# Causal attention on one core: the mask of the maxima added by TensorE, and the values of two halves issued together

## The reference

```
x = x + 0.5 * ffn(layernorm(x))
x = x + attention(layernorm(x))      # 16 heads of 16 features, causal
x = x + 0.5 * ffn(layernorm(x))

attention:  scores = Q K^T / 4, -inf where key > query
            softmax over keys, times V, heads summed through WO
ffn:        256 -> 1024, butterfly (10 stages), gelu, butterfly, 1024 -> 256
```

## Time and profile before

| | |
|---|---|
| time, median of 3 runs | 2121.79 us (2121.55 to 2124.14) |
| the profiled execution, its own time | 2122.12 us |
| its span, first to last instruction | 2120.3 us |
| busy: TensorE, VectorE, ScalarE, GpSimd | 96%, 79%, 64%, 12% |
| mean granted TensorE clock | 0.988 of full speed |

### The profile page before, as it was taken

How to read it: one execution, slowest core, us unless ns; L and a number is a source line. 1 busy time by engine, 2 the same in 40 slices (tenths; PEclk the granted TensorE clock), 3 DMA queues, 4 the chain that set the end, 5 groups by cost and what they waited for, 6 DMA issues and landing times.

```text
span 2120.3 us, 58107 instructions
## 1 busy us (share of the span) xinstructions
PE 2033.0 (96%) x23960; PEld 1207.5 (57%) x23960; DVE 1680.3 (79%) x3588; ACT 1350.4 (64%) x1592; POOL 259.0 (12%) x723
## 2 busy tenths in 40 slices
PE   1699999989999999999999999999999999999999
PEld 1476666555555555555555555555555555568887
DVE  6734444459999999999999999999999999635562
ACT  2423222238888888888888888888888888763222
POOL 8300000001111111111111111010110111100000
PEclk8799999999999999999999999999999999999999
DMA  7011211121211111111111111111111111101110
GB/s 202 22 48 47 86 52 51 47 61 44 51 42 45 41 43 49 42 46 41 44 47 42 46 43 44 46 42 46 43 44 45 42 46 33 50 24 60 60 40 21
DMA packets 89976, 104.19 MB, mean 49 GB/s; under 512 B 21264, under 2 KB 52592, under 8 KB 89456
## 3 DMA queue, kind: packets, MB, share of 16 engines
q1 hardware_dynamic: 89008, 100.23, 16.6%
q0 software_dynamic: 704, 0.25, 0.2%
HBM read 70.54 MB, written 29.36 MB: 47 GB/s over the span
## 4 chain that ended last, share of the span: by engine, by line
PE 92%; DVE 4%; ACT 2%; issue 1%; SPq 1%; DMA 0%; ACTq 0%; DVEq 0%
PE PS L1067 31%; PE PS L1189 30%; PE PS L1048 12%; PE PS L1025 6%; PE PS L1169 6%; PE PS L1120 3%; PE PS L1042 1%; DVE OA L781 1%; PE PS L991 1%; DVE BNS L718 1%; DVE OA L771 1%; ACT PG L606 0%; ACT L583 0%; SPq L367 0%; ACT OA L591 0%
## 5 line engine op out<-in xcount | busy, mean ns | idle before, releaser
L667 ACT ACTIVATE PG<-PS 128x1024 f32<-128x1024 f32 (+1 forms) x1152 | 1119.5, 978 | 248.0 <-PE PS L1169 186.3
L880 DVE TENSOR_REDUCE MXP<-PS 128x1 f32<-128x512 f32 x1792 | 1106.5, 686 | 35.7 <-PE PS L1067 34.8
L1067 PE MATMUL PS<-KT,QT 48*128 48x512 f32 (+3 forms) x2304 | 821.0, 431 | 5.6 <-DVE MXP L880 3.1
L1169 PE MATMUL PS<-QT,KT 50*128 50x512 f32 (+1 forms) x2304 | 810.0, 431 | 0.0
L1189 PE MATMUL PS<-PG,VH 128*17 128x128 f32 x16896 | 725.9, 276 | 0.1
L1189 PEld LDWEIGHTS PS<-PG,VH 128*17 128x17 f32 x16896 | 400.1, 96 | 414.5 <-issue 364.1
L1067 PEld LDWEIGHTS PS<-KT,QT 48*128 48x128 f32 x2304 | 345.8, 184 | 271.8 <-DVE MXP L880 129.9
L1169 PEld LDWEIGHTS PS<-QT,KT 50*128 50x128 f32 x2304 | 339.3, 184 | 10.3 <-issue 9.9
L876 DVE CUSTOM_DVE_ANT_0 PS<-PS,MASK 128x128 f32<-128x128 f32 (+3 forms) x512 | 249.9, 505 | 83.0 <-PE PS L1067 75.6
L551 POOL TENSOR_SCALAR_AFFINE_SELECT PG<-PG 128x128 f32<-128x128 f32 x512 | 137.3, 294 | 1005.4 <-ACT PG L667 1005.2
L1048 PE MATMUL PS<-MD,PG 128*128 128x256 f32 x1024 | 244.1, 388 | 4.9 <-DVE X L845 3.4
(11 more groups left out here) (101 smaller groups left out, 899.2 us busy)
## 6 DMA issues: line engine op xcount, KB each, us to landing
KT<-k_parts SPq DMA_DIRECT2D x256, 64.0 KB
QT<-q_parts SPq DMA_DIRECT2D x256, 64.0 KB
q_parts<-OA SPq DMA_DIRECT2D x16, 512.0 KB, 2.7
k_parts<-OA SPq DMA_DIRECT2D x16, 512.0 KB, 2.7
KT<-k_parts SPq DMA_DIRECT2D x256, 32.0 KB
QT<-q_parts SPq DMA_DIRECT2D x256, 32.0 KB
o_parts<-OS SPq DMA_DIRECT2D x128, 64.0 KB
OA<-o_parts SPq DMA_DIRECT2D x32, 256.0 KB
```

The costliest lines, as they stand in the source:

```text
L667: nc.scalar.activation(PB[n % 2][half][:, :, q0:TILE], PS[:, half * 1024:half * 1024 + 1024].rearrange("p (k q) -> p k q", k=2)[:, :, q0:T ...
L880: nc.vector.tensor_reduce(dst, bank(b), AX.X, ALU.max).then_inc(mx_red, 1)
L1067: mm(bank(4 + qs % 2 if b is None else b, w), NQ[0:SC, (BT * place(j) + qs) * P:(BT * place(j) + qs + 1) * P].bitcast(f32r), NK[0:SC, c * ...
L1169: last = mm(PS[:, (2 * half + k) * 512 + q0:(2 * half + k + 1) * 512], CK[0:SM, kb * P:(kb + 1) * P].bitcast(f32r), CQ[0:SM, place(j) * TI ...
```

## The change

In attention TensorE adds the causal mask to a diagonal maximum: behind the matmul of the maximum, which leaves its accumulation open, comes a second matmul into the last 128 columns, the bf16 identity (identb) times the 128 x 128 triangle of MASK. VectorE then reduces it with a plain tensor_reduce of (qs + 1) x 128 columns. The 28 diagonal maxima made before attention keep VectorE's masked instruction.

The second half of the values of a chunk moves one slot on, to just before the first half of the next chunk's values, so that both are issued together; only for the last chunk of a query tile (c = 0, ends_tile) it stays at the end of its slot. pv_done becomes two semaphores, one for each half, and each exponential waits for its own.

```diff
-        pv_done = sem("pv_done")
+        pv_done = [sem("pv_done0"), sem("pv_done1")]
...
+        def ends_tile(n):
+
+            return CH[n % NCH][1] == 0
@@ GpSimd, copy_v @@
-                    pool.wait_ge(pv_done, (h - 1) * NCH + CH.index((NT - 1, c)) + 1 + FREE_PB)
+                    pool.wait_ge(pv_done[1], (h - 1) * NCH + CH.index((NT - 1, c)) + 1 + FREE_PB)
@@ ScalarE, exps and take_sums @@
-                act.wait_ge(pv_done, h * NCH + n + 1)
                 for half in range(2):
+                    act.wait_ge(pv_done[half], h * NCH + n + 1)
...
-                act.wait_ge(pv_done, h * NCH + LAST[j] + 1 + FREE_PB)
+                act.wait_ge(pv_done[1], h * NCH + LAST[j] + 1 + FREE_PB)
@@ VectorE, maximum @@
-                b = 4 + qs % 2 if b is None else b
+                first = b is None
+                b = 4 + qs % 2 if first else b
                 dve.wait_ge(mx_ps, seq + 1)
                 dst = MXP[:, BT * place(j) + qs, c:c + 1]
-                if j == c:
-                    w = (qs + 1) * P
+                w = (qs + 1) * P if j == c else TILE
+                if j == c and first:
...
-                    nc.vector.tensor_reduce(dst, bank(b), AX.X, ALU.max).then_inc(mx_red, 1)
+                    nc.vector.tensor_reduce(dst, bank(b, w), AX.X, ALU.max).then_inc(mx_red, 1)
@@ TensorE, maximum @@
-                mm(bank(4 + qs % 2 if b is None else b, w), NQ[0:SC, (BT * place(j) + qs) * P:(BT * place(j) + qs + 1) * P].bitcast(f32r),
-                   NK[0:SC, c * TILE:c * TILE + w].bitcast(f32r), start=True, stop=True).then_inc(mx_ps, 1)
+                dst = bank(4 + qs % 2 if b is None else b, w)
+                alone = j != c or b is None
+                last = mm(dst, NQ[0:SC, (BT * place(j) + qs) * P:(BT * place(j) + qs + 1) * P].bitcast(f32r),
+                   NK[0:SC, c * TILE:c * TILE + w].bitcast(f32r), start=True, stop=alone)
+                if not alone:
+                    last = mm(dst[:, qs * P:(qs + 1) * P], identb[:, :], MASK[:, 3 * P:4 * P], start=False, stop=True)
+                last.then_inc(mx_ps, 1)
@@ TensorE, values @@
-                if half:
-                    last.then_inc(pv_done, 1)
+                last.then_inc(pv_done[half], 1)
@@ TensorE, the loop over slots @@
                 ahead_maximum(n, 1)
+                if n > 1 and not ends_tile(n - 2):
+                    values(*divmod(n - 2, NCH), 1)
                 if n:
                     values(*divmod(n - 1, NCH), 0)
...
                 ahead_maximum(n, 3)
-                if n:
+                if n and ends_tile(n - 1):
                     values(*divmod(n - 1, NCH), 1)
```

More of the change, by code:

```diff
@@ L975, in _ @@
             pe.sem_inc(y_ps, 1)
-            pe.sem_inc(pv_done, FREE_PB)
+            for half in range(2):
+                pe.sem_inc(pv_done[half], FREE_PB)
             pe.wait_ge(a_up, 1)
```

## The result

The changed kernel takes 2303.81 us (2301.76 to 2306.87, 4 runs) beside 2121.67 us before: ratio 1.0857, 95% interval 1.0838 to 1.0876. It is 182 us slower; the forecast was 194 slower, 2316, in a range of 2250 to 2360.

What follows compares the result with a forecast made beforehand. The prediction took TensorE's order to set the pace, with VectorE just behind. From 2122 us it took 148 for the merge, added 136 for the bank wait and 206 for the masks: 2316 us, range 2250 to 2360.

Steps and rivals of the forecast that it cites:

- The merge: Attention's values of two halves issued together save 0.33 us in each of 448 slots, a slot of 2.12 us: -148 us.
- a TensorE that waits for exponentials: Sign of being wrong: in the profile after, idle ScalarE is replaced by TensorE waiting for exponentials.
- The bank wait: Fourth maximum in a row waits for the first's reduction in three banks, 0.59 us at 230 slot borders: +136 us.
- the wait view: Sign of being right: idle time of TensorE's maxima loads put down to VectorE's reductions grows by over 100 us.
- The masks: Full-height mask matmuls break the groups of pairs in 121 diagonal slots, 3.82 us each, 1.70 over 2.12: +206 us.
- the term m: Time of a mask from its load to the next load in masked slots: 0.215 us, bounds 0.14 and 0.25.
- VectorE's relief: Dropping 484 masked maxima and their accumulator reads frees 60 us of VectorE in slots where it waits already: 0.
- Banks that don't hold TensorE: Rival: in the merged order VectorE keeps pace with bursts of maxima, so no bank wait: 2180 us; chance 0.08.
- Masks that don't break groups: Rival: in diagonal slots a mask costs its 0.05 us and pairs stay together: 2134, up to 2200 us; chance 0.05.
- VectorE as the limit: Rival: VectorE limits masked slots and its relief pays -0.5 us x 121 = -60: 2062 us; chance 0.04.
- More waits than counted: Rival: row transposes in the long groups, or masked slots with late exponentials, add waits: 2360 us and over; chance 0.03.

Runs made afterwards that it cites:

- e1: The changed kernel without masks on TensorE: values merged, VectorE masks the diagonal maxima as before; 2222.03 us, ratio 1.0476 to the kernel before.
- e2: The changed kernel with the values in the order of before, so only the masks on TensorE; 2270.06 us, ratio 1.0696 to the kernel before.
- e7: As e2, but each mask made of two matmuls of 64 rows on the partitions of the maxima; 2153.27 us, ratio 1.0149 to the kernel before.
- e4: The kernel before, with VectorE reducing only 128 of 512 columns of attention's maxima off the diagonal; 2116.31 us, ratio 0.9975.
- e3: The merged values of e1 with the short reductions of e4; 2098.80 us, ratio 0.9894 to the kernel before.
- e14: e3 with the masked maxima too reduced over their first 128 columns only; 2068.89 us, ratio 0.9746 to the kernel before.
- e13: Kernel before with values merged at every second border, maximum 1 behind double blocks, and the short reductions of e4; 2146.29 us, ratio 1.0107.

## Why the prediction was right

**The sum.** 2122 - 148 + 136 + 206 = 2316; measured 2304. Both large terms are confirmed as mechanisms. e1 by the prediction's own prices (28 borders with a wait, for there are no masks beside them) should be +106 and is +101; e2, with the mask at the 0.16 us that the changed kernel shows, should be +155 and is +149.

**The merge, -148.** Right in size where nothing waits: 2.13 us between double blocks without maxima, for a forecast of 2.12. But every other slot there takes 2.33, since the exponentials, named as next, came in already. The prediction had a TensorE that waits for exponentials among the signs of being wrong; it came only here, where the whole merge is worth a few us.

**The bank wait, +136.** Every link of a plain slot was measured as forecast (0.54, 1.28, 0.43, 0.99 for 1.00). It was made of rows of before in which a maximum stood alone, and held in the middle of attention. What I expected of the wait view was too much: idle time before the maxima's loads that is put down to reductions went from 107.2 to 192.5 us, by 85 and not by over 100. That view starts to count only when TensorE has nothing left, so it isn't the price of a late load:

```profile
PEld PS L1075 <- DVE MXP L885: 192.5, 664, 0.5
...
PEld PS L1075 <- issue: 87.8, 335, 0.6
```

**The masks, +206.** The mechanism was right: a full-height matmul breaks the pairs. Here a size was off, the term m. I took the row transpose's 0.215 us; a mask has 0.162. 484 x 0.053 = 26 us, so the term is +180 and the sum 2290. Measured is 14 us more. The trace shows two places that could make them up. The row transposes, 30 in the stretch with maxima, cost 0.45 us more each than before, 14 us at most (at half of them the sum already has a wait); the prediction had them at nothing and named them only in its last rival. And in the last slots the sum credits the merge with 17 x 0.33 = 6 us, where it gave 22 x 0.14 = 3. This is an estimate; no run takes the transposes away. So the sum came within 12 us partly by luck: a mask priced too high hid the waits that were left out.

The rule of the Trainium skill that a change of tiling mode drains TensorE (TensorEngine Tiling (Array Packing), Key Properties) agrees with these traces: 0.16 us a mask for 0.058 of columns, and e7, whose masks stay in the maxima's mode, at a fifth of e2's price. So does the rule on weights that aren't fp32 (TensorE: Matmul & The Clock Gate, Weight-path perf modes), in direction: a mask's load has 0.10 us in the trace, a full fp32 load 0.19, and the estimate of 0.20 for m from that page was nearer than the row I took, though still above 0.162.

**VectorE's relief, 0.** Right. e4 takes more than two fifths off VectorE's time and gains 5 us. And the relief wasn't even had: its busy time stayed at 1285 us, because reductions that don't follow one another closely no longer overlap (a mean of 684 ns each and 1138.9 / 1824 = 0.624 us busy, 0.615 before), and the diagonal ones now take 0.28 us to 0.56 for their 128 to 384 columns; with 0.68 for 512 that is 1.94 us a slot, where the prediction took some 1.6.

```profile
L885 DVE TENSOR_REDUCE MXP<-PS 128x1 f32<-128x512 f32 x1824 | 1138.9, 684 | 103.7 <-PE PS L1075 77.8 <-PE PS L1078 25.2
...
L885 DVE TENSOR_REDUCE MXP<-PS 128x1 f32<-128x384 f32 x120 | 66.9, 557 | 115.7 <-PE PS L1078 115.7
...
L885 DVE TENSOR_REDUCE MXP<-PS 128x1 f32<-128x128 f32 x120 | 33.6, 280 | 0.0
```

Here the idle time tells who is late now: 115.7 us before the 384-column reductions end with a mask.

**The rivals.** Banks that don't hold TensorE: out by e3 and e14. Masks that don't break groups: out by e2 and e7. VectorE as the limit: out by e4. More waits than counted: true on a small scale, at the row transposes, and far from its 2360.

## What to carry to other kernels

An engine that is 96% busy and not the limit leaves no room for a new order: before work is grouped, follow one buffer around its loop (load, first use, release, next load) and add the block that the grouping puts into it. A small matmul that fills the array in another shape than its neighbours costs its way in and out and the overlap of those neighbours, here 1.2 to 1.5 us a slot for 0.2 us of columns. And with one wait removed by an experiment, look for the next one before you promise the gain: e13, with VectorE's work cut down, was still a loss, by my reading through the exponentials. Count, too, everything that takes a turn of the same buffers: here a row transpose did.

## What was not expected of the hardware

Two matmuls of 64 rows in the maxima's part of the array ran beside the scores at 0.11 us of load for both, and 31 us remained of 149. Fewer instructions on VectorE didn't lower its busy time in the changed kernel: reductions that follow each other start every 0.60 us (four in 2.48 us), lone ones have their full 0.68. And a bf16 mask matmul behind another of its kind took 0.058 us.
